# Causal mask of the second attention: added on VectorE from PSUM instead of by two matmuls on TensorE

## The chip, the cores and the metric

The kernel runs on one core of one Trainium2 chip. The metric is the time of one execution on the device in microseconds (us); lower is better. Before the change it is 649.9 us, the median of three runs (648.09 to 652.0).

## The reference

The input x has 128 sequences of 32 tokens with 256 features. Two layers follow one another. The first is an attention with 16 heads and no mask, behind an RMS norm that is scaled and shifted by a condition, with normalised q and k. The second takes its output as the hidden state h and computes this (the second attention is the one with the causal mask):

```
x1     = rmsnorm(h, ln1_w)
scores = einsum("bqhd,bkhd->bhqk", q(x1), k(x1)) / sqrt(16)
scores = where(tril(ones(32, 32)), scores, finfo.min)
probs  = softmax(scores)
attn   = einsum("bhqk,bkhd->bqhd", probs, v(x1)) @ Wo.T
mod    = 0.1 * tanh(attn @ A)
u      = rmsnorm(h, ln2_w)
gate   = silu(u @ W_in.T + mod * (u @ A) @ B)
out    = x + h + (gate * (u @ W_up.T)) @ W_down.T
```

## The kernel before

Tokens are taken in 16 blocks of 256 (two tiles of 128 tokens, t = 0 and 1; a tile holds four sequences). Most products are made of three matmuls, with each operand split into a high and a low part. Names tell the part of the work: `x_` loads and normalises, `a_` is the first attention, `o_` and `r_` its output and residual, `b_` the second attention, `m_` its modulation, `f_` the gated network in four pairs of chunks (0 to 3), and `h`, `l` in tile names stand for high and low.

Nothing is planned at run time. Three lists written out by hand give the order: START (blocks 0 to 3 fill up), ORDER (the body of the loop over positions 4 to 13, each entry with a shift: -1 is the block before), and END. Each engine walks through the same list and takes the entries that are its own, so an engine's queue is strictly in that order, and an entry that waits holds all behind it on its engine. Semaphores `done[name]` count the entries that are finished. TensorE (PE) and SyncE (SP) have the lists unrolled.

The second attention of a block goes like this. PE makes q and k (`b_q`, `b_k`) into the two PSUM banks `b_banks`, ScalarE (ACT) copies them out (`b_q_out`, `b_k_out0` to `3`). `b_scores` on PE first multiplies an identity in bf16 (`identb`) with a mask in bf16 (`maskb`) into both banks, 512 columns each (line 657), and then adds 64 small matmuls onto it (line 506). VectorE (DVE) runs `b_shift1` and `b_shift0`, each for one tile: the maximum over the keys (line 911) and the difference from it (line 914), both read from PSUM, the second into `zb` in SBUF. ACT takes the exponential in place (`b_exp`, line 858), DVE the sum and its reciprocal (`b_rowsum`, lines 919 and 921), GpSimd (POOL) scales by it (`b_weigh`, line 1118), DVE transposes (`b_flip`, line 925), and `b_pv` on PE (line 671) multiplies with the values `vj`. These were moved across partitions before: `b_v_out1` on ACT (lines 853 and 854) ends the copy of the values, and `b_move` on SP then issues 16 DMAs (line 469). `m_turn` on PE (line 680) writes into the second of the banks and waits for both `b_shift`.

Around it in ORDER, in the queues of the single engines: on PE `f_gate2`, `b_scores`, (next position) `a_turn1`, `a_turn0`, `f_up2`, `f_down0`, `f_gate3`, `a_v`, `a_scores`, `f_up3`, `f_down1`, `f_down2`, `b_pv`, `x_turn`, `f_up0`, `a_pv0`. On ACT `f_tanh2`, `x_norm1`, `b_v_out1`, `f_hi1`, `a_k_out0`, `b_exp1`, `a_k_out3`, `b_exp0`, `a_k_out2`, `x_norm0`, `a_k_out1`, `a_q_out`, `f_tanh3`, `f_hi2`. On DVE `f_half2`, `b_shift1`, `b_shift0`, `b_rowsum1`, `b_rowsum0`, `f_mul2`, `b_flip1`, `b_flip0`, `f_half3`, `a_shift1`. On POOL `f_lo1`, `b_weigh1`, `b_weigh0`, `f_lo2`, where `f_lo` (line 1123) subtracts the high part from the product, from SBUF to SBUF. `a_scores` (line 506 too, into `a_banks`) waits for `a_q_out` and the four `a_k_out`.

A few more lines of DVE that the text speaks of: line 1075 `f_half`, 1082 `f_mul`, 1039 `o_lo` and 1063 in `m_mul` (both read two tensors in SBUF).

Of the kernel before, what the change touches and what calls it, by code (L numbers as in the profile page):

```python
# [44 lines left out]
    ("a_flip0", 0), ("m_mul", -1), ("a_pv0", 0), ("a_pv1", 0), ("x_scale", 1), ("m_turn", -1), ("x_shift", 1),  # L45
    ("o_odd", 0), ("m_out", -1), ("o_even", 0), ("f_down3", -2), ("o_hi", 0), ("f_gate0", -1), ("x_hi", 1),
# [35 lines left out]
    ("a_weigh0", 1), ("r_add", 0), ("b_weigh1", 0), ("masks", 0), ("b_weigh0", 0), ("lo", 9), ("lo", 10),  # L82
    ("a_shift1", 1), ("b_exp1", 0), ("a_v_out", 1), ("b_exp0", 0), ("load", 2), ("x_shift", 2), ("x_lo", 2),
    ("hi", 11), ("a_shift0", 1), ("a_rowsum1", 1), ("b_v0", 0), ("load", 3), ("a_scale1", 2), ("a_scale0", 2),
    ("a_rowsum0", 1), ("b_shift0", 0), ("b_shift1", 0), ("a_flip1", 1), ("a_flip0", 1), ("hi", 12), ("o_odd", 1),
    ("load", 4), ("b_v1", 0), ("x_square", 3), ("b_scores", 0), ("o_hi", 1), ("load", 5), ("m_tanh", 0),
# [100 lines left out]
def bass_adaln_attention_ffn(nc, x, condT, w_emb, b_emb, g_norm, w_qkv, gq, gk, w_out, ln1, ln2,  # L187
# [5 lines left out]
    with ExitStack() as ctx:  # L193
# [11 lines left out]
        wdn = [sb(f"wdn_{s}", [P, FC, D], F32R) for s in ("hi", "lo")]  # L205
        b3 = sb("b3", [96, FF], F32R)
        ident = sb("ident", [P, P])
        identb = sb("identb", [P, P], BF16)
        causal = sb("causal", [P, S])
        maskb = sb("maskb", [P, H, S], BF16)  # L210
        heads = sb("heads", [P, 8])
# [960 lines left out]
```

## Time and profile before

| what | value |
|---|---|
| median of 3 runs | 649.9 us |
| profiled execution | 646.44 us, of it 644.6 us span from first to last instruction |
| mean granted TensorE clock | 0.973 of full speed |
| PE busy | 600.9 us (93%) |
| DVE busy | 462.1 us (72%) |
| ACT busy | 370.0 us (57%) |
| POOL busy | 221.1 us (34%) |
| chain that ended last | PE 75%, issue of DMAs by SP 10%, DVE 6% |

The busy time of an engine is the sum of its instructions. The chain is followed back from the last instruction, at each step to what released it. The loop runs from about 142 to 536 us, with a distance of about 35.9 us from one position to the next.

### The profile page before, as it was taken

What the parts mean: (1) busy time and instruction counts of PE and PEld (TensorE: products, weight loads), DVE (VectorE), ACT (ScalarE), POOL (GpSimd) and SP (SyncE); (2) the same over time, 40 slices, a digit from 0 to 9 for tenths busy, and PEclk for the clock granted to TensorE, in tenths of its full rate; (3) what the DMA queues carried; (4) which work ended last, traced back from release to release, by engine and by line L of the source; (5) the groups of instructions that cost most, each with busy time, mean ns of one, the idle gap of its engine ahead of it and who ended that gap; (6) DMA issues with size and microseconds to landing.
All of it is one profiled execution on the core that took longest, in us unless ns stands there. A gap on an engine that the chain in (4) does not pass through costs nothing.

```text
span 644.6 us, 22549 instructions
## 1 busy us (share of the span) xinstructions
PE 600.9 (93%) x9112; PEld 558.6 (87%) x9128; DVE 462.1 (72%) x1070; ACT 370.0 (57%) x803; POOL 221.1 (34%) x196
## 2 busy tenths in 40 slices
PE   9565789899999999999999999999999999999997
PEld 8544679788999999999999999999999998888997
DVE  4567878577686777777786767777787766976452
ACT  3647656474565748475665747474656657473531
POOL 1221323415153443424242444334242533523132
PEclk9956799899999999999999999999999999999999
DMA  6322200000201002010101001010101010010000
GB/s 181 90 82 82 71 20 23 14 21 17 67 18 49 19 4 60 11 53 16 50 18 51 19 14 50 8 56 13 51 18 50 18 35 15 7 39 15 27 25 34
DMA packets 31961, 24.35 MB, mean 38 GB/s; under 512 B 7632, under 2 KB 30800, under 8 KB 31872
## 3 DMA queue, kind: packets, MB, share of 16 engines
q1 hardware_dynamic: 31328, 22.36, 11.8%
q8 instruction: 73, 1.20, 0.8%
q10 hardware_dynamic: 544, 0.66, 0.4%
q14 instruction: 16, 0.13, 0.1%
HBM read 14.61 MB, written 4.19 MB: 29 GB/s over the span
## 4 chain that ended last, share of the span: by engine, by line
PE 75%; SPq 10%; DVE 6%; issue 4%; ACT 2%; DMA 2%; POOL 1%; POOLq 0%; ACTq 0%; DVEq 0%
PE gate_bank L494 12%; PE up_bank L494 11%; PE down_bank L718 10%; SPq L469 10%; PE b_banks L494 7%; PE a_banks L486 7%; PE x_bank L486 6%; PE a_banks L609 4%; PE b_banks L486 3%; PE b_banks L506 2%; PE gate_bank L704 2%; PE a_banks L506 2%; PE up_bank L533 2%; DMA vj<-vs 2%; PE b_banks L671 2%
## 5 line engine op out<-in xcount | busy, mean ns | idle before, releaser
L1123 POOL TENSOR_TENSOR gl<-gu,gh 128x512 fp32r<-128x512 f32 x64 | 83.1, 1299 | 117.9 <-ACT gh L877 117.7
L1075 DVE SCALAR_TENSOR_TENSOR th<-th,gate_bank 128x512 f32<-128x512 f32 x64 | 43.2, 675 | 46.8 <-ACT th L872 46.8
L494 PE MATMUL up_bank<-uh,wup_hi 128*128 128x256 f32 x256 | 76.3, 298 | 0.0
L1111 POOL TENSOR_TENSOR qk<-qk,rx 128x512 f32<-128x512 f32 x32 | 33.3, 1060 | 123.6 <-DVE rx L903 123.6
L718 PE MATMUL down_bank<-wdn_hi,gh 128*128 128x256 f32 x256 | 74.1, 290 | 0.6 <-POOL gl L1123 0.6
L494 PE MATMUL gate_bank<-uh,win_hi 128*128 128x256 f32 x256 | 72.4, 283 | 0.2
L718 PE MATMUL down_bank<-wdn_hi,gl 128*128 128x256 f32 x256 | 72.1, 282 | 0.0
L718 PE MATMUL down_bank<-wdn_lo,gh 128*128 128x256 f32 x256 | 72.1, 282 | 0.0
L494 PE MATMUL up_bank<-ul,wup_hi 128*128 128x256 f32 x256 | 71.9, 281 | 0.0
L494 PE MATMUL up_bank<-uh,wup_lo 128*128 128x256 f32 x256 | 71.9, 281 | 0.0
L494 PE MATMUL gate_bank<-ul,win_hi 128*128 128x256 f32 x256 | 71.4, 279 | 0.0
L494 PE MATMUL gate_bank<-uh,win_lo 128*128 128x256 f32 x256 | 71.4, 279 | 0.0
L1118 POOL TENSOR_TENSOR za<-za,ria 128x512 f32<-128x512 f32 x32 | 33.0, 1051 | 80.5 <-DVE ria L921 80.5
L872 ACT ACTIVATE th<-gate_bank 128x512 f32<-128x512 f32 x64 | 38.3, 598 | 37.7 <-PE gate_bank L704 34.6
L877 ACT ACTIVATE gh<-gu 128x512 fp32r<-128x512 f32 x64 | 40.3, 631 | 27.7 <-DVE gu L1082 19.6
L494 PEld LDWEIGHTS up_bank<-uh,wup_hi 128*128 128x128 f32 x256 | 48.8, 191 | 2.7 <-issue 2.5
L1082 DVE TENSOR_TENSOR gu<-th,up_bank 128x512 f32<-128x512 f32 x64 | 42.9, 670 | 9.4 <-PE up_bank L494 6.6
L718 PEld LDWEIGHTS down_bank<-wdn_hi,gh 128*128 128x128 f32 x256 | 48.3, 189 | 1.4 <-POOL gl L1123 0.9
L494 PEld LDWEIGHTS gate_bank<-uh,win_hi 128*128 128x128 f32 x256 | 48.2, 188 | 1.4 <-issue 0.8
L494 PEld LDWEIGHTS up_bank<-ul,wup_hi 128*128 128x128 f32 x256 | 49.0, 191 | 0.0
L494 PEld LDWEIGHTS up_bank<-uh,wup_lo 128*128 128x128 f32 x256 | 48.7, 190 | 0.0
L494 PEld LDWEIGHTS gate_bank<-ul,win_hi 128*128 128x128 f32 x256 | 48.1, 188 | 0.4
(157 smaller groups left out, 1844.4 us busy)
## 6 DMA issues: line engine op xcount, KB each, us to landing
xa<-in_x SPq DMA_DIRECT2D x16, 256.0 KB, 3.6
xres<-in_x SPq DMA_DIRECT2D x16, 256.0 KB, 2.9
vj<-vs SPq DMA_DIRECT2D x256, 16.0 KB
out<-outb SPq DMA_DIRECT2D x16, 256.0 KB, 3.2
stage<-in_w_inT SPq DMA_DIRECT2D x2, 512.0 KB, 3.6
stage<-in_w_upT SPq DMA_DIRECT2D x2, 512.0 KB, 4.2
stage<-in_w_downT SPq DMA_DIRECT2D x2, 512.0 KB, 4.0
stage<-in_w_qkv SPq DMA_DIRECT2D x2, 384.0 KB, 4.9
```

The costliest lines, as they stand in the source:

```text
L469: sp.dma_start(vj[32 * j:32 * j + 32, b].rearrange("p t r -> p (t r)"), vs2[32 * b:32 * b + 32, u].rearrange("p t r -> p (t r)")).then_inc ...
L486: mm = pe.matmul(dst, stat[a][:, k, t * P:(t + 1) * P], w[b][:, k, c0:c1], start=(k == 0 and j == 0), stop=(k == KT - 1 and j == 2))
L494: mm = pe.matmul(dst, w[a][:, k, c0:c0 + P], mov[b][:, k, :], start=(first and k == 0 and j == 0), stop=(last and k == KT - 1 and j == 2), ...
L506: mm = pe.matmul(place(t, m, b, g), stat(t, m)[rows, 32 * b:32 * b + 32], mov(t, m)[rows, P * b:P * b + P], start=start, stop=True, skip_g ...
L718: mm = pe.matmul(Db[:, t * D:(t + 1) * D], stat[a], wdn[b][:, 2 * c + i, :], start=(c + t + i + j == 0), stop=(c == PAIRS - 1 and i == 1 a ...
L872: act.activation(th[:, :, :].rearrange("p c n -> p (c n)"), Gb[:, :], ACT.Tanh, scale=0.5).then_inc(f_tanh, 1)
L877: act.activation(gh[:, c % 2], gu[:, c % 2], ACT.Copy).then_inc(f_hi, 1)
L1075: dve.scalar_tensor_tensor(out=whole, in0=whole, scalar=1.0, in1=Gb[:, :], op0=ALU.add, op1=ALU.mult).then_inc(f_half, 1)
L1082: dve.tensor_tensor(gu[:, c % 2].rearrange("p c n -> p (c n)"), th[:, :, :].rearrange("p c n -> p (c n)"), Ub[:, :], ALU.mult).then_inc(f_ ...
L1111: pool.tensor_tensor(heads_of, heads_of, rx[:, 32 * t:32 * t + 32].unsqueeze(2).to_broadcast([P, 2 * H, HD]), ALU.mult).then_inc(done[name ...
L1118: pool.tensor_tensor(z[:, t], z[:, t], ri[:, t, :].unsqueeze(2).to_broadcast([P, H, S]), ALU.mult).then_inc(done[name], 1)
L1123: pool.tensor_tensor(gl[:, c % 2], gu[:, c % 2], gh[:, c % 2].bitcast(F32), ALU.subtract).then_inc(f_lo, 1)
```

## The change

The two mask matmuls of `b_scores` go, with `identb`, `maskb` and the entry `masks` that filled them. All matmuls of the scores now overwrite (`start=True`). A new entry `b_mask0` or `b_mask1` stands on DVE directly in front of each `b_shift` in all three lists. It adds `causal` (float32, broadcast over the heads) to the scores as it reads them from PSUM and writes `zb`. `b_shift` then takes the maximum of `zb` and subtracts it in place, from SBUF to SBUF. `m_turn` waits for the two `b_mask` and no longer for the two `b_shift`. No other entry changes its place.

```diff
 ORDER = [
-    ("x_load", 2), ("x_norm1", 1), ("f_half2", -2), ("b_v_out1", -1), ("a_turn1", 0), ("b_shift1", -1),
-    ("f_hi1", -2), ("b_move", -1), ("a_turn0", 0), ("f_up2", -2), ("a_k_out0", 0), ("f_lo1", -2), ("b_shift0", -1),
+    ("x_load", 2), ("x_norm1", 1), ("f_half2", -2), ("b_v_out1", -1), ("a_turn1", 0), ("b_mask1", -1),
+    ("b_shift1", -1), ("f_hi1", -2), ("b_move", -1), ("a_turn0", 0), ("f_up2", -2), ("a_k_out0", 0), ("f_lo1", -2),
+    ("b_mask0", -1), ("b_shift0", -1), ("b_exp1", -1), ("f_down0", -2), ("a_k_out3", 0), ("b_rowsum1", -1),
...
-                    for bank in range(2):
-                        pe.matmul(Bb[:, bank, :], identb[:, :], maskb[:, :, :].rearrange("p h s -> p (h s)"),
-                                  start=True, stop=False, skip_group_check=True)
                     scores(b_place, lambda t, m: q2T[:, m, t, :],
-                           lambda t, m: k2p[:, m, t].rearrange("p b h s -> p (b h s)"), False).then_inc(done[name], 1)
+                           lambda t, m: k2p[:, m, t].rearrange("p b h s -> p (b h s)")).then_inc(done[name], 1)
...
-                    wait(pe, done["b_shift0"], n)
-                    wait(pe, done["b_shift1"], n)
+                    wait(pe, done["b_mask0"], n)
+                    wait(pe, done["b_mask1"], n)
...
+                if name[2:-1] == "mask":
+
+                    wait(dve, done["b_scores"], n)
+                    wait(dve, done[f"b_flip{t}"], n - 1)
+                    if isinstance(n, int) and n == 0:
+                        dve.wait_ge(loaded["causal"], 16)
+                    dve.tensor_tensor(z[:, t].rearrange("p (g c) s -> p g c s", g=4), sc(t),
+                                      causal[:, :].unsqueeze(1).unsqueeze(1).to_broadcast([P, 4, H // 4, S]),
+                                      ALU.add).then_inc(done[name], 1)
+                elif name == f"b_shift{t}":
+                    wait(dve, done[f"b_mask{t}"], n)
+                    dve.tensor_reduce(mx[:, t, :], z[:, t], AX_X, ALU.max).then_inc(maxed[x][t], 1)
+                    wait(dve, maxed[x][t], n)
+                    dve.tensor_tensor(z[:, t], z[:, t], mx[:, t, :].unsqueeze(2).to_broadcast([P, H, S]),
+                                      ALU.subtract).then_inc(done[name], 1)
```

## Rows read from the trace of the kernel before

**Rows 1.** Busy time by windows: length, busy PE, PEld, DVE, ACT, POOL, PE clock, DMA.

```profile
357.10:393.10 36.00, 35.73 (x565) 33.41 (x566) 27.05 (x64) 22.15 (x49) 13.96 (x13) 1.00 0.10 32
```

**Rows 2.** Chain of waits, a position of the loop: start, duration, engine and work.

```profile
365.79 1.09 PE a_banks L506 x64
...
371.33 0.67 PE b_banks L671 x52
```

**Rows 3.** Chain of waits, the position three before.

```profile
250.83 0.08 ACT ha L854
...
261.88 1.76 DMA vj<-vs
...
263.77 0.73 PE b_banks L671 x50
```

**Rows 4.** Timeline of SP, the DMAs of b_move: start, duration of the group.

```profile
215.25 10.76 SPq L469 DMA_DIRECT2D vj<-vs  x16
...
250.97 11.51 SPq L469 DMA_DIRECT2D vj<-vs  x16
...
358.75 10.81 SPq L469 DMA_DIRECT2D vj<-vs  x16
...
502.37 10.89 SPq L469 DMA_DIRECT2D vj<-vs  x16
```

**Rows 5.** Timeline of PE's weight loads around the mask.

```profile
357.13 0.12 PEld L657 LDWEIGHTS b_banks<-maskb,identb 128*128 128x128 bf16 x2
357.67 0.92 PEld L506 LDWEIGHTS b_banks<-k2p,q2T 64*32 64x32 f32 x64 [0.42 <-issue]
```

**Rows 6.** Groups by form on DVE: count, then busy, mean ns, idle before.

```profile
L914 DVE TENSOR_TENSOR zb<-b_banks,mxb 128x512 f32<-128x512 f32 x32 | 22.1, 692 | 1.6
...
L911 DVE TENSOR_REDUCE mxb<-b_banks 128x16 f32<-128x512 f32 x32 | 21.9, 684 | 8.3 <-PE b_banks L506 8.3
```

**Rows 7.** Timeline of DVE behind the scores.

```profile
357.96 0.69 DVE L1075 SCALAR_TENSOR_TENSOR th<-th,gate_bank 128x512 f32<-128x512 f32 x1 [1.59 <-ACT th L872]
358.93 0.69 DVE L911 TENSOR_REDUCE mxb<-b_banks 128x16 f32<-128x512 f32 x1 [0.29 <-PE b_banks L506]
359.66 0.69 DVE L914 TENSOR_TENSOR zb<-b_banks,mxb 128x512 f32<-128x512 f32 x1
360.27 0.68 DVE L911 TENSOR_REDUCE mxb<-b_banks 128x16 f32<-128x512 f32 x1
...
366.93 0.69 DVE L911 TENSOR_REDUCE mxa<-a_banks 128x16 f32<-128x512 f32 x1 [0.92 <-PE a_banks L506]
```

**Rows 8.** Timeline of ACT in the same stretch.

```profile
361.71 0.63 ACT L858 ACTIVATE zb<-zb 128x512 f32<-128x512 f32 x1
...
363.79 0.69 ACT L792 ACTIVATE q1T<-a_banks,gcol 128x512 f32<-128x512 f32 x1
```

**Rows 9.** Timeline of POOL in the same stretch.

```profile
359.27 1.29 POOL L1123 TENSOR_TENSOR gl<-gu,gh 128x512 fp32r<-128x512 f32 x1 [1.27 <-ACT gh L877]
```

**Rows 10.** Timeline of POOL and of DVE, an earlier stretch.

```profile
158.41 2.99 POOL L1123 TENSOR_TENSOR gl<-gu,gh 128x512 fp32r<-128x512 f32 x2 [3.36 <-ACT gh L877]
...
158.74 1.50 DVE L1039 TENSOR_TENSOR ol<-o,oh 128x512 fp32r<-128x512 f32 x1
```

**Rows 11.** Single lines of DVE: duration ns min/median/max, first and last start.

```profile
L1063 DVE SCALAR_TENSOR_TENSOR m<-th,ha x16: 181/652/1273, 83.1 to 618.9; 128x32 f32<-128x32 f32 x16
...
L1039 DVE TENSOR_TENSOR ol<-o,oh x16: 648/693/1575, 44.4 to 589.3; 128x512 fp32r<-128x512 f32 x16
```

**Rows 12.** Chain of waits behind the loop.

```profile
541.34 0.70 DVE mxb L911
...
550.54 0.87 PE a_banks L609 x53
```

**Rows 13.** Timeline of DVE and of PE behind b_pv.

```profile
372.72 0.71 DVE L925 STREAM_TRANSPOSE pTa<-za 128x512 f32<-128x512 f32 x1 [0.17 <-POOL za L1118]
...
373.89 0.31 PE L609 MATMUL a_banks<-pTa,vs 32*32 32x64 f32 x12
```

More of the change, by code:

```diff
@@ L35 @@
 ORDER = [
[9 rows of a table removed]
-    ("a_flip0", 0), ("m_mul", -1), ("a_pv0", 0), ("a_pv1", 0), ("x_scale", 1), ("m_turn", -1), ("x_shift", 1),
-    ("o_odd", 0), ("m_out", -1), ("o_even", 0), ("f_down3", -2), ("o_hi", 0), ("f_gate0", -1), ("x_hi", 1),
[7 rows of a table removed]
[10 rows of a table added]
+    ("m_turn", -1), ("x_shift", 1), ("o_odd", 0), ("m_out", -1), ("o_even", 0), ("f_down3", -2), ("o_hi", 0),
+    ("f_gate0", -1), ("x_hi", 1), ("o_lo", 0), ("x_lo", 1), ("r_mm", 0), ("f_tanh0", -1), ("f_half0", -1),
+    ("a_qk1", 1), ("f_mul0", -1), ("r_square", 0), ("a_qk0", 1), ("r_rms", 0), ("a_square1", 1), ("a_copy1", 1),
+    ("f_gate1", -1), ("f_hi0", -1), ("f_lo0", -1), ("r_norm0", 0), ("r_norm1", 0), ("f_out", -2), ("a_sum1", 1),
+    ("r_load", 0), ("r_turn", 0), ("f_up1", -1), ("f_store", -2), ("r_hi", 0), ("f_tanh1", -1), ("r_lo", 0),
[4 rows of a table added]
 ]
@@ L81 @@
     ("ld_b_emb", 0), ("x_load", 2), ("ld_wo_a", 0), ("a_exp0", 1), ("b_v_out1", 0), ("a_weigh1", 1), ("ld_g", 0),
[L82 to L85, printed above, removed]
@@ L86 @@
-    ("load", 4), ("b_v1", 0), ("x_square", 3), ("b_scores", 0), ("o_hi", 1), ("load", 5), ("m_tanh", 0),
-    ("f_lo0", 0), ("x_load", 3), ("a_v", 1), ("x_turn", 2), ("load", 6), ("x_hi", 2), ("ld_causal", 0),
-    ("b_rowsum1", 0), ("b_rowsum0", 0), ("lo", 11), ("a_pv0", 1), ("a_pv1", 1), ("f_up0", 0), ("b_flip1", 0),
-    ("b_flip0", 0), ("o_even", 1), ("x_scale", 2), ("o_lo", 1), ("r_square", 1), ("a_weigh0", 2), ("a_square0", 2),
-    ("a_weigh1", 2), ("load", 7), ("m_out", 0), ("r_norm1", 1), ("r_norm0", 1), ("lo", 12), ("a_copy1", 2),
@@ L91 @@
-    ("load", 8), ("r_hi", 1), ("a_square1", 2), ("m_mul", 0), ("r_rms", 1), ("f_tanh0", 0), ("a_copy0", 2),
-    ("b_k_out1", 1), ("a_sum0", 2), ("r_add", 1), ("r_lo", 1), ("a_sum1", 2), ("b_pv", 0), ("r_mm", 1),
[8 rows of a table removed]
-    ("r_load", 0), ("r_turn", 1), ("b_rowsum0", 1), ("o_even", 2), ("o_odd", 2), ("a_scale1", 3), ("f_gate0", 0),
[4 rows of a table removed]
-    ("m_tanh", 1), ("load", 12), ("a_copy0", 3), ("a_copy1", 3), ("m_out", 1), ("f_lo1", 1), ("x_load", 4),
-    ("b_move", 0), ("a_weigh0", 3), ("vd_zero", 0), ("r_square", 2), ("x_norm0", 4), ("x_norm1", 4), ("a_rms", 3),
@@ L108 @@
-    ("f_up2", 0), ("a_v", 2), ("f_gate3", 0), ("r_load", 1), ("x_turn", 3), ("f_down0", 0), ("f_up3", 0),
-    ("b_weigh1", 2), ("f_down1", 0), ("a_pv0", 2), ("a_pv1", 2), ("a_qk1", 3), ("r_rms", 2), ("a_qk0", 3),
-    ("f_half0", 1), ("f_out", 0), ("b_pv", 1), ("x_lo", 4), ("f_down2", 0), ("r_lo", 2), ("f_tanh0", 1),
[7 rows of a table removed]
+    ("a_weigh0", 1), ("r_add", 0), ("b_weigh1", 0), ("b_weigh0", 0), ("lo", 9), ("lo", 10), ("a_shift1", 1),
+    ("b_exp1", 0), ("a_v_out", 1), ("b_exp0", 0), ("load", 2), ("x_shift", 2), ("x_lo", 2), ("hi", 11),
@@ new lines @@
+    ("a_shift0", 1), ("a_rowsum1", 1), ("b_v0", 0), ("load", 3), ("a_scale1", 2), ("a_scale0", 2),
+    ("a_rowsum0", 1), ("b_mask0", 0), ("b_shift0", 0), ("b_mask1", 0), ("b_shift1", 0), ("a_flip1", 1),
+    ("a_flip0", 1), ("hi", 12), ("o_odd", 1), ("load", 4), ("b_v1", 0), ("x_square", 3), ("b_scores", 0),
+    ("o_hi", 1), ("load", 5), ("m_tanh", 0), ("f_lo0", 0), ("x_load", 3), ("a_v", 1), ("x_turn", 2), ("load", 6),
+    ("x_hi", 2), ("ld_causal", 0), ("b_rowsum1", 0), ("b_rowsum0", 0), ("lo", 11), ("a_pv0", 1), ("a_pv1", 1),
@@ new lines @@
+    ("f_up0", 0), ("b_flip1", 0), ("b_flip0", 0), ("o_even", 1), ("x_scale", 2), ("o_lo", 1), ("r_square", 1),
+    ("a_weigh0", 2), ("a_square0", 2), ("a_weigh1", 2), ("load", 7), ("m_out", 0), ("r_norm1", 1), ("r_norm0", 1),
+    ("lo", 12), ("a_copy1", 2), ("load", 8), ("r_hi", 1), ("a_square1", 2), ("m_mul", 0), ("r_rms", 1),
[10 rows of a table added]
+    ("b_rowsum0", 1), ("o_even", 2), ("o_odd", 2), ("a_scale1", 3), ("f_gate0", 0), ("b_k", 1), ("b_q", 1),
[5 rows of a table added]
+    ("vd_zero", 0), ("r_square", 2), ("x_norm0", 4), ("x_norm1", 4), ("a_rms", 3), ("f_up2", 0), ("a_v", 2),
[10 rows of a table added]
@@ L497, in feature_major, with scores @@
                 return mm
-            def scores(place, stat, mov, start):
+            def scores(place, stat, mov):
                 for t in range(TB):
@@ L506, in scores @@
                                 mm = pe.matmul(place(t, m, b, g), stat(t, m)[rows, 32 * b:32 * b + 32],
[L507 removed]
+                                               mov(t, m)[rows, P * b:P * b + P], start=True, stop=True,
                                                skip_group_check=True)
@@ L1030, in do @@
                     softmax(name, n, "a", a_scores_of, za, pTa, mxa, rsa, ria)
-                elif name[:2] == "b_" and name[2:-1] in ("shift", "rowsum", "flip"):
+                elif name[:2] == "b_" and name[2:-1] in ("mask", "shift", "rowsum", "flip"):
                     softmax(name, n, "b", b_scores_of, zb, pTb, mxb, rsb, rib)
```

28 lines of the change are left out of this document (9 added, 19 removed), and 112 rows, old and new, of tables (END, ORDER, START).

## The prediction

> **What bounds the kernel now.** I read the busy time by windows first. In one position of the loop PE is busy for 35.73 of 36.00 us at full clock, DVE for 27.05, ACT for 22.15 and POOL for 13.96 [rows 1]. That looks like a kernel that is bound by PE alone, so that whatever is taken off PE would be gained. The chain of waits says something narrower. In one position it runs through PE from end to end, and `b_pv` (line 671) follows the matmuls before it at 371.33 [rows 2]. Three positions earlier it leaves PE: it goes from the last copy of the values on ACT (250.83) through SP's 16 issues, and the DMA that starts at 261.88 and takes 1.76 us ends just before `b_pv` at 263.77 [rows 3]. So there are two chains of nearly one length between the scores and `b_pv`. The SP timeline says how near. The 16 issues take 10.76, 10.81 or 10.89 us in some positions and 11.51 in others [rows 4]; of the nine groups from 215.25 to 502.37, five are short ones and four long ones, in turn. The issues of rows 3 end at 250.97 + 11.51 = 262.48, and `b_pv` starts 1.29 us later. I measure both chains from the start of the mask's weight load, m = 357.13 [rows 5]. PE reaches `b_pv` at m + 14.20 [rows 2]. The DMA chain starts at m + 1.62 [rows 4] and allows `b_pv` at 1.62 + 10.81 + 1.29 = m + 13.72 in a short position, at 1.62 + 11.51 + 1.29 = m + 14.42 in a long one. The DMA chain begins with the copies on ACT that queue behind `f_tanh2`, which waits for `f_gate2`, the work of PE just in front of the mask. The mask matmuls are therefore not in that chain, and removing them doesn't shorten it.
>
> **PE, what goes.** The mask's weight loads start at 357.13 and those of the scores at 357.67 [rows 5]: 0.54 us for each block, 16 x 0.54 = 8.6 us in all. If no wait took its place, the short positions would gain 14.20 - 13.72 = 0.48 us each and the long ones nothing, 5 x 0.48 = 2.4 us, since the DMA chain then sets `b_pv`. That is the most that the loop can gain. The 64 score matmuls stay as they are; that they overwrite instead of adding I cost at nothing, as the same line into `a_banks` does it at the same rate.
>
> The Trainium skill (TensorE: Matmul & The Clock Gate, section "Wait — 56ns, not 53.3ns?") gives 215.7 ns from start to start for 512 columns at full clock, by which the two would be an estimated 0.43 us and not 0.54, or 6.9 us for 16 blocks; the sum would hardly move, as little of it is gained either way.
>
> **DVE, what comes.** Before, a tile takes a maximum and a difference, 684 and 692 ns [rows 6], with 0.73 us from the start of the one to that of the other, which waits for it, and 0.61 to the next tile [rows 7]. After, a tile is sum, maximum, difference. The sum reads PSUM and one SBUF tensor like the old difference: 0.69. Maximum and difference now read SBUF: the nearest row for an operation with both operands there is `o_lo`, median 693 ns, minimum 648 [rows 11]; I take 0.69 again, 0.65 and 0.72 bound it. One more step of 0.72 for each tile, 1.4 us for a block, on an engine that idles for about 9 us of 36 [rows 1]. On load alone this is free. What counts is who waits behind it.
>
> The Trainium skill (VectorE: DVE Perf Modes, section "The TRN2 errata") has a table with 58 fixed cycles for a source in SBUF and 120 for one in PSUM. By it maximum and difference would get some 0.06 us shorter each, an estimated 0.25 us for a block, or 4 us of DVE time in all. The median of 693 ns from SBUF beside 692 from PSUM [rows 6, 11] speaks against it.
>
> **A lock that the difference now meets.** The old difference read PSUM and took 692 ns whatever POOL did. Line 1039, which reads two SBUF tensors, has a maximum of 1575 ns beside its median of 693 [rows 11]. One such case: it starts at 158.74, with POOL's line 1123 at work since 158.41; at 1.29 us each [rows 9] the first of the two POOL operations ends at 159.70, and the DVE one ends at 160.24, 0.54 us later, as if it had run only then [rows 10]. Line 1063, on 32 elements, takes 181 ns at best and 652 in the median for the same reason. The new difference reads `zb` and `mxb`, two SBUF tensors. The Trainium skill (SBUF — State Buffer, section "SBUF: two separate sides") tells of a port pair of VectorE and GpSimd that one holds for its whole instruction when VectorE reads two SBUF tensors. The trace agrees, with those numbers.
>
> **The loop, step by step.** `f_half2` runs at 357.96 as before, since `f_tanh2` holds it, and the next DVE operation can start 0.61 later. So `b_mask1` starts at 358.57 and not at 358.93 - 0.54 [rows 7]: 0.36 us of PE's 0.54 arrive here. Maximum at 359.30. The difference wants 360.02, but POOL's `f_lo1` runs from 359.27 to 360.56 [rows 9], and it ends at 361.11. Then `b_mask0` at 361.03, maximum 361.76, difference 362.48 to 363.17. `b_exp0` on ACT started at 361.71 [rows 8]; now at 363.20, 1.49 us later. Behind it in ACT's queue stand `a_k_out2`, `x_norm0`, `a_k_out1` and `a_q_out`, which ended at 363.79 + 0.69 = 364.48 [rows 8] and now ends at 365.97. PE's `a_scores` waits for these. Its weight loads started 0.08 before 365.79 [rows 2], at 365.71; now at 366.03 at the earliest, 0.32 later, although PE could be there 0.54 earlier. This is the wait that takes the place of the mask. `b_pv` then comes at m + 14.20 + 0.32 = 14.52 by PE. Short positions: 14.52 for 14.20, +0.32. Long ones: 14.52 for 14.42, +0.10. 5 x 0.32 + 4 x 0.10 = +2.0 us for the loop. The bounds: without the lock the difference of the second tile ends 0.47 earlier, `a_scores` starts 0.15 before its old time, and the loop gains 5 x 0.15 = 0.8 us.
>
> What the later DVE work does: `b_rowsum1` and all up to `f_half3` come about 1.5 us later, of which the 0.92 us that DVE waited for `a_scores` at 366.93 [rows 7] swallows most; `a_shift1` starts some 0.5 late. `a_flip0` ended at 372.72 + 0.71 = 373.43, and PE's `a_pv0`, which waits for it, started at 373.89 [rows 13]: 0.46 of cover, and PE itself is 0.32 late, so I cost this at nothing. `b_weigh` on POOL, `f_lo2` and `f_tanh3` come 1.5 late with their users further off. `m_turn` waits for less than before; at nothing. SP issues the same DMAs, and nothing moves past them.
>
> **The first blocks.** Block 1's mask stands with nothing but PE around it and is worth up to 0.54 us, of which the later transposes give about half back. In block 0 the scores are done before DVE comes to them, so all of its 1.4 us is added to a full queue; about 0.6 gets through. Bounds -1.1 (two blocks' 0.54) to +1.4; I take +0.3, nearer the middle because both go through the same DVE. The entry `masks` that goes had no one waiting on it: nothing.
>
> **The last blocks.** Behind the loop the chain runs through DVE, from the first `b_shift` of block 13 at 541.34 on to `a_pv0` at 550.54 [rows 12], through the six steps in place of four: +1.4, less the 0.54 by which PE lets DVE start earlier: +0.9. In block 15 DVE meets no POOL operation, and `f_mul2` behind the softmax comes 1.4 - 0.36 = 1.0 later; `f_up3` on PE, which waits for it and has some 0.7 of cover, is about 0.35 late. Together +1.2; bounds 0 and +2.8.
>
> **Sum.** +2.0 + 0.3 + 1.2 = +3.5 us. The sum is made against the profiled execution: 646.44, which is its span of 644.6 and 1.8 around it, becomes 649.9. The median of the runs lies 3.5 us above that execution; I carry this distance over, and 649.9 becomes 653.4 us. A measurement of this kernel tells about 0.5% (3.2 us) from no change, so the forecast stands on that edge.
>
> **The rivals.**
> - *PE's time is gained* (faster). It needs `b_pv` to have no DMA chain behind it and `a_scores` no ACT queue: 649.9 - 8.6 = 641.3. The point from which it decides: 16 issues in under 13.66 - 1.62 - 1.29 = 10.75 us in every position, and DVE's six steps done before 362.3. Rows 3 and 4 speak against it: 0.04.
> - *The lock doesn't hit the difference* (POOL and DVE don't meet, or the new form isn't held). Loop -0.8, ends +1.5: +0.7, 650.6: 0.17.
> - *DVE becomes the pace.* `a_flip0` or `f_mul3` runs out of cover: if DVE is 0.5 us later than I reckon, with 0.46 of cover at `a_pv0` [rows 13] partly spent, some 0.3 us comes on top in each of 10 positions, and as much in the ends: +6.5 to +8, 657: 0.17.
> - *The change doesn't shorten PE's queue* (the slot of the mask fills with the start of the scores). The loop is held by `a_q_out` anyway; the ends lose 0.5 to 1 more: 654.2: 0.04.
> - The forecast, 651.0 to 655.5, has the remaining 0.58.
>
> **How the numbers follow.** Of the forecast's 0.58 some 0.28 lies within 0.5% and 0.30 above. Faster: 0.04 + 0.01 = 0.05. Same: 0.28 + 0.16 = 0.44. Slower: 0.30 + 0.17 + 0.04 = 0.51. The range takes in the forecast, the case without the lock and most of the DVE case: 649.0 to 657.5.
>
> **What the profile would show.** `b_pv` 14.5 us behind the start of the scores' block in all positions, and no longer in turn 14.2 and 14.4. A wait of PE for ACT's `q1T` of about 0.8 us in each position. The difference of the first tile at 1.1 us and that of the second at 0.69. If the first is 0.69 too, the lock step is wrong. If PE waits for `vj` and not for `q1T`, the ACT step is wrong. If the period falls by 0.5 us, the DMA chain was no bound.

## The result, and the profile of the changed kernel

The changed kernel is slower by 1.3%: 657.8 us in the median (653.8 to 662.8) beside 649.0 for the kernel before, ratio 1.0127 with an interval of 1.0086 to 1.0168. Run again beside the last experiments it gave 659.8 us and 1.0167 (1.013 to 1.0205). The sign was forecast, the size was not: 3.5 us were reckoned, and 8.8 came, 11.2 in the repetition. At the ratio of the first measurement the forecast's 649.9 us becomes 658.2, just above the range's upper end of 657.5.

The profiled execution took 658.1 us, of it 656.3 us span, at a mean granted clock of 0.964. The page of the changed kernel, busy times and the chain that ended last:

```profile
PE 600.6 (92%) x9096; PEld 561.2 (86%) x9096; DVE 485.2 (74%) x1100; ACT 370.6 (56%) x803; POOL 221.8 (34%) x196
...
PE 66%; DVE 17%; issue 7%; ACT 6%; POOL 2%; SPq 2%; DMA 0%; ACTq 0%; POOLq 0%; DVEq 0%
```

DVE has 23 us more work, as reckoned, and PE is busy as long as before although the mask matmuls are gone; more of its work ran at half clock (the mean granted clock was 0.973 before). The chain has changed hands: PE and SP's issues have given up 9 and 8 points of it, and DVE's share went from 6% to 17%. One position of the loop by windows (the columns of [rows 1]):

```profile
328.00:364.00 36.00, 35.11 (x564) 33.14 (x562) 28.86 (x66) 22.23 (x49) 13.75 (x13) 1.00 0.11 31
```

PE now lacks 0.9 us of 36 where it lacked 0.3. The three DVE steps of a tile, groups by form (count, busy, mean ns of one, idle before), answer to [rows 6]:

```profile
L916 DVE TENSOR_TENSOR zb<-zb,mxb 128x512 f32<-128x512 f32 x32 | 26.6, 830 | 1.1
L914 DVE TENSOR_REDUCE mxb<-zb 128x16 f32<-128x512 f32 x32 | 22.0, 687 | 1.1
L909 DVE TENSOR_TENSOR zb<-b_banks,causal 128x512 f32<-128x512 f32 x32 | 21.8, 682 | 3.8 <-PE b_banks L507 3.8
```

Sum and maximum take what was put in for them. The difference takes 830 ns in the mean, and the timeline says why. DVE and POOL in the loop, which answer to [rows 7] and [rows 9]:

```profile
365.42 0.68 DVE L909 TENSOR_TENSOR zb<-b_banks,causal 128x512 f32<-128x512 f32 x1
366.12 1.29 POOL L1129 TENSOR_TENSOR gl<-gu,gh 128x512 fp32r<-128x512 f32 x1 [1.27 <-ACT gh L873]
366.13 0.69 DVE L914 TENSOR_REDUCE mxb<-zb 128x16 f32<-128x512 f32 x1
366.86 1.10 DVE L916 TENSOR_TENSOR zb<-zb,mxb 128x512 f32<-128x512 f32 x1
...
369.31 0.69 DVE L916 TENSOR_TENSOR zb<-zb,mxb 128x512 f32<-128x512 f32 x1
```

The first difference lasts until 367.96, 0.55 us past the end of POOL's operation; the second has no such neighbour. In nine of the ten positions, blocks 4 to 12, the first one is 0.40 to 0.42 longer than 0.69. The chain of waits through the same position, from there to `b_pv`, and the waits of PE and of its weight loads over the whole span (us, times, longest):

```profile
370.04 0.04 ACT zb L854
...
372.22 0.59 ACT q1T L788
...
372.85 1.16 PE a_banks L507 x64
...
378.46 0.67 PE b_banks L667 x51
```
```profile
PEld a_banks L507 <- ACT q1T L788: 9.2, 11, 0.9
PE a_banks L507 <- ACT q1T L788: 7.0, 11, 0.7
```

The scores' weight loads begin at 364.07 here, so `a_scores` comes 8.78 us and `b_pv` 14.32 us after them. (This `b_pv` is the start of its first matmul in the timeline, 378.39. The chain counts it from the end of the matmul ahead, 378.46.) In the kernel before, the same distances from the mask's load were 8.58 and 14.1 to 14.5 in turn. Now they are 8.78 and 14.29 to 14.34 for all blocks from 4 to 12 (8.41 and 13.94 for block 3, whose difference met no POOL operation).

Something else in that chain was in no step of the forecast. Behind `b_pv`, in the middle of the 128 small matmuls of `a_pv`:

```profile
381.93 0.72 PE a_banks L610 x45
382.65 0.95 issue
383.61 0.34 PE a_banks L610 x13
383.95 0.35 PE b_banks L676 x2
384.31 2.42 PE down_bank L714 x12
```

PE stands for 0.95 us with nothing to wait for that the profile shows, and then runs twelve matmuls in 2.42 us that take 1.41 at full clock, as the granted clock fell to 0.5 for 3.41 us. Such stalls stand in five of the ten positions (3.1 us in all), this half clock behind one of them.

To tell where the time went I cut each trace at two places: the scores' first weight load of block 3, and that of block 13 (in kernels with mask matmuls the mask's load, 0.54 us earlier). The ten positions between are split once more, at the first matmul of each `b_pv`. The column `a_pv` says what the ten runs of `a_pv` last together beyond 1.77 us each, which an undisturbed one takes from its first matmul to its last. In us, one profiled execution of each kernel:

```
kernel                            until    ten         up to   from    a_pv   rest    span
                                  block 3  positions   b_pv    b_pv
before                            177.7    358.7       142.6   216.1   0.4    108.2   644.6
changed                           181.7    366.3       142.8   223.5   4.2    108.3   656.3
changed, again                    181.2    367.4       144.0   223.4   2.3    108.3   656.9
mask matmuls kept, DVE adds too   180.5    368.2       144.5   223.7   1.9    109.8   658.5
no mask at all                    175.3    361.3       137.8   223.5   4.4    106.5   643.1
no mask, values copied early      175.0    358.3       136.4   221.9   2.5    106.5   639.8
changed, difference from PSUM     178.1    365.8       139.5   226.4   5.9    108.4   652.3
changed, other order on DVE       179.4    362.5       141.9   220.6   2.7    107.9   649.8
changed, late exponential         179.0    378.6       139.2   239.4   5.7    108.2   665.9
changed, two small matmuls        181.0    363.1       145.6   217.5   0.4    110.1   654.2
other order and small matmuls     180.5    364.0       147.4   216.6   0.6    109.8   654.4
before, values copied early       182.9    356.5       140.8   215.7   0.2    107.4   646.8
changed, values copied early      183.2    361.8       139.5   222.3   2.8    108.2   653.1
the same, PE's program moved      187.5    359.7       139.5   220.2   0.6    108.6   655.8
```

The rest is as before. The loop has 7.6 to 8.6 us more, where 2.0 were reckoned. The forecast reckoned the path up to `b_pv`, and there the changed kernel has 0.2 us more than before (1.4 in the repetition). All else, 7.4 us, is lost behind `b_pv`, and the kernel with no mask at all loses as much there (223.5 for 216.1), without any new work on DVE. (The kernel with both mask forms loses 7.6 us there, but 5.0 of them by a wait of its own.) The first blocks have 4 us more, but their length is no fixed thing: the kernel before, changed only in when it copies the values, has 182.9 there with longer stretches at half clock.

### The profile page after: what moved, and what is told of

Read it like the earlier page. It is cut to its first block, busy times and chain, and to the rows that moved or that the text cites. A ratio compares the mean times of both kernels' runs of the same rounds, so it can differ in the third digit from the quotient of the medians.

```text
span 656.3 us, 22531 instructions
## 1 busy us (share of the span) xinstructions
PE 600.6 (92%) x9096; PEld 561.2 (86%) x9096; DVE 485.2 (74%) x1100; ACT 370.6 (56%) x803; POOL 221.8 (34%) x196
## 4 chain that ended last, share of the span: by engine, by line
PE 66%; DVE 17%; issue 7%; ACT 6%; POOL 2%; SPq 2%; DMA 0%; ACTq 0%; POOLq 0%; DVEq 0%
PE gate_bank L495 10%; PE up_bank L495 10%; PE down_bank L714 10%; PE b_banks L495 7%; PE a_banks L487 6%; PE x_bank L487 4%; PE a_banks L610 4%; DVE mxb L914 3%; DVE zb L909 3%; PE b_banks L487 3%; PE a_banks L507 2%; ACT k1p L797 2%; PE gate_bank L700 2%; PE up_bank L534 2%; SPq L470 2%
## 5 line engine op out<-in xcount | busy, mean ns | idle before, releaser
L1124 POOL TENSOR_TENSOR zb<-zb,rib 128x512 f32<-128x512 f32 x32 | 34.0, 1080 | 53.6 <-DVE rib L932 53.6
L495 PEld LDWEIGHTS gate_bank<-uh,win_lo 128*128 128x128 f32 x256 | 49.2, 192 | 0.0
```

Of the source, the lines that this page charges most:

```text
L495: mm = pe.matmul(dst, w[a][:, k, c0:c0 + P], mov[b][:, k, :], start=(first and k == 0 and j == 0), stop=(last and k == KT - 1 and j == 2), ...
L1124: pool.tensor_tensor(z[:, t], z[:, t], ri[:, t, :].unsqueeze(2).to_broadcast([P, H, S]), ALU.mult).then_inc(done[name], 1)
```

## The experiments

**Only the DVE half.** The two mask matmuls go back in front of the scores, and DVE still adds.

```diff
+                    for bank in range(2):
+                        pe.matmul(Bb[:, bank, :], identb[:, :], maskb[:, :, :].rearrange("p h s -> p (h s)"),
+                                  start=True, stop=False, skip_group_check=True)
                     scores(b_place,
```

> The DVE part alone: the two mask matmuls stay in PE's queue (the scores then overwrite them), DVE adds the mask as in the changed kernel. Theory A (two causes: the wait of a_scores for a_q_out, and stalls of PE inside a_pv that come from where PE's program is cut, as it is 4 instructions a block shorter): PE's program is as in the kernel before, so the long gaps inside a_pv (0.5 to 1.2 us in every second block of the changed kernel) are gone; b_exp0 starts where it did in the changed kernel, since POOL's f_lo1 holds the first difference to the same moment; distance of the positions even, 36.0 us, loop +1 us on before, whole 650 to 653 us, ratio 1.002 to 1.007. Theory B (DVE's later work makes those gaps too): the gaps stay, the loop is as long as in the changed kernel or longer, ratio 1.012 to 1.02.

661.3 us, ratio 1.0203 (1.0157 to 1.025). It is the slowest but two of all. Theory B had a loop and a ratio like these, but neither theory had the place. The chain of waits shows a place that nobody had looked at, the last step of the norm of the residual (`r_rms`), and the timeline shows its neighbour:

```profile
354.99 0.17 DVE nr_t L902
355.17 0.02 issue
355.19 1.29 DVE rr L906
...
356.50 0.48 ACT tok L830
```
```profile
355.17 1.28 POOL L1141 TENSOR_TENSOR gl<-gu,gh 128x512 fp32r<-128x512 f32 x1 [3.88 <-ACT gh L880]
355.19 1.28 DVE L906 SCALAR_TENSOR_TENSOR rr<-nr_t,nr_y 128x2 f32<-128x2 f32 x1
```
```profile
PE x_bank L630 <- ACT tok L830: 5.0, 5, 1.2
```

An operation on two columns, 0.17 us otherwise, takes 1.28 because a POOL operation began 0.02 us before it, and PE waits for the result in every second position, 5.0 us in all (the last line, waits of PE from 180 to 540 us). So what the later DVE work costs depends on which short steps it pushes into POOL's operations. Two more things went against theory A. The stalls inside `a_pv` are still there in two positions (blocks 4 and 12) although PE's program is as long as before. And as the scores come 0.54 us later, the first difference meets only the end of POOL's operation: it takes 0.69 to 0.73 us in the loop and not 1.1.

**Only the PE half.** The mask matmuls go and nothing comes in their place.

```diff
-                    for bank in range(2):
-                        pe.matmul(Bb[:, bank, :], identb[:, :], maskb[:, :, :].rearrange("p h s -> p (h s)"),
-                                  start=True, stop=False, skip_group_check=True)
```

> The PE part alone: no mask matmuls and no mask on DVE; b_shift reads PSUM as before. The kernel leaves the causal mask out. Theory A: the short positions gain up to 0.5 us and the long ones nothing (DMA chain to b_pv), at most -2.4 us in the loop, but the gaps inside a_pv are there as in the changed kernel, +3 us or more with what they cost in clock: 647 to 652 us. Theory B: no gaps inside a_pv, loop -2.4 us, ends -1 to -2: 645 us, ratio 0.992 to 0.996. The count by PE alone would be -8.6 us: 640.5 us.

648.0 us, 0.9987 (0.995 to 1.0024): of PE's 8.6 us nothing that can be measured arrives. The chain of waits has the DMA of the values in front of `b_pv` again, and the waits of PE in the loop are these:

```profile
259.50 1.75 DMA vj<-vs
261.25 0.14 issue
261.39 0.73 PE b_banks L666 x50
```
```profile
PE a_banks L609 <- issue: 2.8, 4, 1.0
PE b_banks L666 <- DMA vj<-vs: 0.9, 3, 0.3
```

The first line of the waits is the stall inside `a_pv`. It comes with no DVE change at all.

The DMA chain is not what takes PE's gain, though. The scores of this position start here:

```profile
247.45 0.65 PEld L506 LDWEIGHTS b_banks<-k2p,q2T 64*32 64x32 f32 x47
```

`b_pv` comes 13.94 us behind them, in a position for which the forecast had the DMA chain hold it at 14.42. From block 4 on no group of the 16 issues takes more than 11.13 us, where four took 11.3 to 11.6 before; why is not shown. Over the ten positions 4.8 of PE's 5.4 us arrive at `b_pv` (137.8 for 142.6), and PE waits for the DMA for 0.9 us. Then 7.4 us are lost behind `b_pv`, 4.0 of them inside `a_pv` and some 1.4 by a half clock behind a stall. Of the expectation, theory A's time and stalls are right, and its 2.4 us at most for the loop is too little: undisturbed distances are 35.3 to 35.7 us where they were 35.7 to 36.1.

**The same with the values copied early**, `b_v_out1` directly behind `b_q_out`, so that SP can issue some 1 us sooner; and **the kernel before with that alone**.

```diff
-    ("b_v_out1", -1), ("a_turn1", 0),
+    ("a_turn1", 0),
...
-    ("b_q_out", 0), ("b_scores", 0),
+    ("b_q_out", 0), ("b_v_out1", 0), ("b_scores", 0),
```

> The PE part alone (no mask matmuls, no mask on DVE; the causal mask is left out) with b_v_out1 early as in the run before. If the DMA chain ate PE's gain: each position is 0.54 us shorter than in the run with the early b_v_out1 that keeps the mask matmuls, 35.2 us, less what the gaps in a_pv take (about 3 us in the loop); 5 us less than that run without them, 2 us less with them. If the DMA chain was not what ate it: 35.7 us as there.

> The kernel before with one edit: b_v_out1 stands right behind b_q_out in ACT's queue and no longer behind f_tanh2, so that the DMA chain to b_pv starts about 1.5 us earlier. If that chain is what holds b_pv in the long positions: no wait for vj, even positions of 35.7 us, loop 1 to 1.5 us shorter, ratio 0.997 to 0.999. If not: no change.

Without mask: 641.9 us, 0.99 (0.9848 to 0.9951), undisturbed distances of 35.2 us. With the mask as before: 648.8 us, 0.9975 (0.9938 to 1.0012), and ten distances of 35.6 to 35.8 where they had gone from 35.7 to 36.1. The even distances show the DMA chain: with it they go in turn, without it they don't, and the loop of the kernel before is 2.2 us shorter without it. By the medians the mask on PE is worth 0.75% with that chain out of the way (0.99 against 0.9975) and 0.1% with it, but the intervals overlap, so the two are not told apart. The traces say that the mask's time arrives at `b_pv` either way (4.4 us without the chain, 4.8 with it) and is lost behind it either way (6.2 and 7.4 us). So in the profiled executions the loop with neither mask nor chain is 1.8 us longer than that with the mask, where 2 to 5 us less were expected.

**The lock taken away by the operand.** The difference reads the scores from PSUM again, the sum still runs.

```diff
-                    dve.tensor_tensor(z[:, t], z[:, t], mx[:, t, :].unsqueeze(2).to_broadcast([P, H, S]),
+                    dve.tensor_tensor(z[:, t].rearrange("p (g c) s -> p g c s", g=4), sc(t),
+                                      mg.unsqueeze(3).to_broadcast([P, 4, H // 4, S]),
```

> The changed kernel with the difference read from PSUM and not from zb, so that it has only one tensor in SBUF; m_turn waits for the two b_shift again. The array that is added is all zeros, so the causal mask is left out; the same instructions run. If POOL's f_lo1 holds the difference because that reads two SBUF tensors: it takes 0.69 us right behind the maximum and not 1.1 to 1.7, a_scores starts 0.4 us earlier (8.35 us behind the start of the scores and not 8.78), the loop is 1 to 2 us shorter than in the changed kernel. If something else held it: same place as in the changed kernel. The gaps inside a_pv stay in both.

654.5 us, 1.0079 (1.0052 to 1.0107). Groups by form:

```profile
L917 DVE TENSOR_TENSOR zb<-b_banks,mxb 128x512 f32<-128x512 f32 x32 | 22.1, 692 | 1.1
```

692 ns where it was 830, `a_scores` 8.37 us after the scores instead of 8.78, and PE's wait for `q1T` in the loop 2.8 us instead of 6.6. The stalls inside `a_pv` stay (3.7 us). The loop was to be 1 to 2 us shorter than in the changed kernel and is 0.5 shorter: 3.3 us are gained up to `b_pv`, and 2.9 are lost behind it, where eight of the ten `a_pv` last 2.05 to 3.18 us and not 1.77.

**The lock taken away by the order.** DVE runs sum and maximum of both tiles first (both stand in `b_mask` here), then both differences.

```diff
-    ("b_mask1", -1), ("b_shift1", -1), ..., ("b_mask0", -1), ("b_shift0", -1),
+    ("b_mask1", -1), ("b_mask0", -1), ("b_shift1", -1), ..., ("b_shift0", -1),
```

> The changed kernel with DVE's six steps in another order: sum and maximum of the one tile, sum and maximum of the other, then the two differences. The first difference then comes when POOL's f_lo1 is over and should take 0.69 us, no step waits for the one just before it except the maxima; b_exp0 starts about 0.6 us earlier, a_scores 8.2 us behind the start of the scores and not 8.78; 2 to 4 us shorter than the changed kernel, ratio 1.005 to 1.009. If the cost is in the number of steps alone and not in the meeting with POOL: within 1 us of the changed kernel.

653.1 us, 1.0056 (1.0024 to 1.0088). In the groups by form the difference takes 683 ns in the mean. `a_scores` comes 8.61 to 8.64 us after the scores, where 8.2 were expected. The loop is 3.8 us shorter than the changed one, but only 0.9 of it is gained up to `b_pv`; the other 2.9 are shorter stalls and no half clock.

So two different means take the lock away, and both kernels are faster than the changed one as it was measured again (1.013 to 1.0205); beside its first measurement (1.0086 to 1.0168) the intervals touch or overlap. What the lock alone costs in the whole is not shown. Positions without a stall keep their 35.9 to 36.1 us in both kernels: what `a_scores` gains, `a_pv` spends again, in gaps too short to be counted as stalls.

**The exponential of the second tile behind `a_q_out`.**

```diff
-    ("b_exp0", -1), ("f_gate3", -2), ...
+    ("f_gate3", -2), ... ("a_q_out", 0), ("b_exp0", -1),
```

> The changed kernel with b_exp0 behind a_q_out in the loop's order, so that the three copies that a_scores waits for no longer stand behind it. If the ACT queue is the wait: a_scores starts 8.1 us behind the start of the scores and PE no longer waits for q1T; b_pv then is held by the DMA chain alone, in turn 13.7 and 14.4 us; loop 1 to 2 us shorter than the changed kernel. If DVE is the pace: b_flip0 and a_flip0 come late, PE waits at a_pv for pTa, no gain or a loss.

666.5 us, 1.0257 (1.0216 to 1.0298). `a_scores` waits for ACT no more (8.01 us after the scores), so that step is right. The expected even `b_pv` at 13.7 and 14.4 us came at 13.6 to 14.1. But DVE's sum over the exponential is held, and all behind it; waits of PE over the span:

```profile
PE up_bank L496 <- DVE gu L1089: 14.1, 21, 1.1
```

This is the rival in which DVE becomes the pace, and it shows how near it lay: 1.1 us of wait at `f_up0` in a position.

**The number of PE's instructions.** Two matmuls of 16 columns ahead of each `b_scores`, which take the place of the mask matmuls in the program though not their time.

```diff
+                    for bank in range(2):
+                        pe.matmul(Bb[:, bank, 0:16], q2T[:, 0, 0, :], k2p[:, 0, 0, 0, 0, 0:16],
+                                  start=True, stop=True, skip_group_check=True)
                     scores(b_place,
```

> The changed kernel with two small matmuls of 16 columns in the place where the mask matmuls stood (the scores overwrite them), so that PE's program has as many instructions for a block as before the change. Theory A (the gaps of 0.5 to 1.2 us in the middle of a_pv come from where PE's program is cut into fetched pieces): the gaps at the same places are gone or moved to others; loop 3 us shorter than in the changed kernel unless they moved to a place that costs as much, ratio to before about 1.008. Theory B (they come from VectorE's side): nothing changes, ratio 1.012 to 1.015.

656.8 us, 1.0115 (1.0068 to 1.0162). In the timeline `a_pv` runs in one piece:

```profile
379.77 1.76 PE L610 MATMUL a_banks<-pTa,vs 32*32 32x64 f32 x127
```

The stalls inside `a_pv` are gone from the loop, and the profiled one is 3.2 us shorter. The median can't be told from that of the changed kernel, and 1.008 was expected. The edit does two things beside its purpose. As fp32, each small matmul has two records (PE has 9160 in the whole and not 9096), so the program is longer than before the change and not as long. And the scores come later, so that the first difference takes 0.73 to 0.82 us and not 1.1: most of the lock is gone too.

**Both together**, the other order on DVE and the small matmuls.

> The changed kernel with two edits at once: DVE's order mask and maximum, mask and maximum, difference, difference, and the two matmuls of 16 columns ahead of the scores. Theory A (the change's cost is a sum of three: the lock on the first difference, PE's stalls inside a_pv, and the added DVE work itself): the first two are gone, the rest is the base distance of about 36.0 us in the loop (10 x 0.13 = 1.3 us more than before) and what the first and last blocks add, some 1 to 3 us together; ratio to before 1.003 to 1.007, no wait of PE named issue inside a_pv, b_pv at 14.3 us from the scores' first weight load. Rival B (the stalls are paid elsewhere anyway, as in the run with the two small matmuls alone, whose ratio stayed at 1.0115): nothing beyond the new order is gained, the ratio is that of the new order or above it by the two matmuls' 0.2 us a block, 1.006 to 1.010.

656.3 us, 1.0099 (1.0065 to 1.0133): in rival B's range and outside theory A's, and no better than the order alone (1.0024 to 1.0088). The stalls in `a_pv` are gone, but the two small fp32 matmuls hold the scores back by 0.47 us (`a_scores` 9.09 us behind the first weight load instead of 8.62), nearly what the mask took, and the position of block 5 loses 0.6 us ahead of `b_pv`. The small matmuls are no free way to move a program.

**The changed kernel again, and with the values copied early.**

> The changed kernel itself once more, beside the two others on the same chip, for a direct comparison. Theory A (what the profile of the changed kernel showed belongs to the program): the first difference again takes 0.40 to 0.42 us longer in at least eight positions, the stalls of PE inside a_pv fall on the same blocks (5, 6, 8, 10, 12), a_scores at 8.78 and b_pv at 14.32 us from the scores' first weight load; ratio 1.009 to 1.017. Rival B (the stalls, the half clock behind one of them and the late first part were chance in that execution): the stalls fall on other blocks or none, and the sum of the ten distances of the loop is below 363 us.

> The changed kernel with b_v_out1 behind b_q_out, so that the DMAs of the values start about 1 us earlier. Theory A (in the changed kernel b_pv is set by the chain through ACT's a_q_out and PE's a_scores, at 14.3 us from the scores, and the DMA chain ended at 13.2 or 13.9 and is hidden): b_pv stays at 14.3 in undisturbed positions, the ratio to before stays at that of the changed kernel, 1.009 to 1.016. Rival B (the DMA chain still ends last now and then): the ratio falls by the 0.25 per cent or more that the same edit brought to the kernel before, to 1.010 or below, and the positions get even.

Again: 659.8 us. The lock is there in the same nine positions, `a_scores` and `b_pv` stand where they stood in all but three of them, and the loop sums to 367.4. The stalls inside `a_pv`, though, are two and not five, in blocks 4 and 12, and the half clock is behind the second. Their place is not fixed by the program alone, and both theories are right in part only. Nor is the loop shorter with fewer stalls: PE waits 0.9 us for `vj` in block 5 and 0.9 us for DVE's `xres` once.

Copied early: 655.1 us, 1.0095 (1.0056 to 1.0135), and an undisturbed distance of 35.63 us, as in the kernel before with the same edit (35.62). The ratio lies in both theories' ranges, but `b_pv` was to stay at 14.3 us by theory A and came at 13.95. DVE and POOL in a position show what it overlooked:

```profile
364.36 1.29 POOL L1145 TENSOR_TENSOR gl<-gu,gh 128x512 fp32r<-128x512 f32 x1 [0.93 <-ACT gh L889]
364.73 0.69 DVE L930 TENSOR_REDUCE mxb<-zb 128x16 f32<-128x512 f32 x1
365.45 0.76 DVE L932 TENSOR_TENSOR zb<-zb,mxb 128x512 f32<-128x512 f32 x1
```

With `b_v_out1` out of ACT's queue, `f_hi1` ends earlier, POOL starts 1.09 us ahead of the difference and not 0.74, and the lock shrinks from 0.41 to 0.07 us here, and to 0.04 in the mean of all 32 differences, where it was 0.14. An ACT entry with no tie to the softmax decided what the DVE step cost.

**PE's program moved as a whole**, on top of that: 20 matmuls of 16 columns ahead of PE's very first.

```diff
+                    if not shifted:
+                        shifted.append(1)
+                        for _ in range(20):
+                            pe.matmul(Ub[0:96, 0:16], mt[:, 0, :], mt[:, 0, 0:16], start=True, stop=True)
```

> The changed kernel with b_v_out1 behind b_q_out (no lock, base distance 35.63 us) and 20 matmuls of 16 columns ahead of the very first ones of PE, where it has nothing to do but wait: they only move the rest of PE's program by 40 instructions. Theory A (the stalls inside a_pv are PE waiting for its own instructions: in the kernels with the shorter program each stall ended 2.3 to 2.8 us after a transfer of 16 KB on the instruction queue had begun, and the transfer began 0.05 us before a_pv at 381.02 in the changed kernel, but 0.93 us before it at 373.89 in the kernel before, where no stall followed): with the program moved by about as much as the mask matmuls of nine blocks had moved it, the transfers begin earlier against a_pv; the stalls of blocks 8 and 12 (1.15 and 1.07 us, and the half clock behind the first, 1.7) are gone or fall on other blocks, the ten distances of the loop sum to 357.5 to 359.5 instead of 361.8, ratio to before 1.002 to 1.006. Rival B (the place in the program has nothing to do with it: the stalls come from what other engines do at that time, or from how many matmuls stand before the scores): the stalls stay in blocks 8 and 12, sum 361 to 363, ratio 1.008 to 1.011.

661.2 us, 1.0213 (1.0182 to 1.0244), outside both theories. PE wasn't idle there, and the timeline shows what the added ones cost (they count double, as fp32, so the program moved by some 80 instructions and not 40):

```profile
1.12 6.58 PE L554 MATMUL up_bank<-mt 128*96 128x16 f32 x40 [1.12 <-DVE mt L963]
```

All first blocks come that much later, which spoils the ratio. The loop is still readable: no stall in `a_pv`, no half clock, a sum of 359.7 instead of 361.8, just above theory A's 359.5. What points to a cause of the stalls is the view of the DMA queues in a short window. First the changed kernel from 380.90 to 381.05, where `a_pv` starts at 381.02 and stalls, then the kernel before from 372.90 to 373.05, where it starts at 373.89 and doesn't (queue, kind: packets, MB, share):

```profile
q8 instruction: 1, 0.02, 50.0%
```
```profile
q8 instruction: 1, 0.02, 40.2%
```

A block of 16 KB of instructions is on its way. In all 14 traces together there are 38 stalls behind the 100th us (over 0.4 us from one weight load of `a_pv` to the next, with nothing waited for), and each of them ended 2.20 to 2.90 us after such a transfer had begun. In every stall of 0.85 us or more in the loop the transfer began within 0.4 us of the start of `a_pv`; in the kernel before, where none is in the loop, it begins 0.9 us or more ahead of that start or 1.0 us behind it. Five runs of `a_pv` in the kernels with moved programs have a transfer within 0.4 us of their start too and no stall, and so has the `a_pv` of block 2 in eight of the others, so that the moment alone doesn't decide.

## Why the prediction was right in its sign and short in its size

**PE's time is not gained: right in the outcome, wrong in the reason.** The kernel without any mask is at 0.9987 (0.995 to 1.0024), so nothing that can be measured arrives. The forecast had the DMA chain take it: at most 2.4 us for the loop, and none in the long positions. In the trace 4.8 us arrive at `b_pv`, in the long positions too, and 7.4 are lost behind it. The DMA chain is real, but it is a cost beside this one: without it the loop is 2.2 us shorter with the mask on PE (358.7 to 356.5) and 3.0 without (361.3 to 358.3). The rival's 641.3 us is near what the kernel with neither mask nor chain takes (641.9), by other terms than the rival's.

**DVE's added step: right.** 682, 687 and 690 ns for sum, maximum and undisturbed difference, beside 0.69. The Trainium skill (VectorE: DVE Perf Modes, section "The TRN2 errata") would have the reads from SBUF shorter by an estimated 0.06 us; the maximum took 687 ns from SBUF and 684 from PSUM, so no run here shows it.

**The lock: right, and now shown.** +0.41 for a forecast of +0.43 (1.09 in all from 360.02 to 361.11, measured 1.10). It goes when the operand is in PSUM and when the order changes, and nearly so when POOL comes earlier or the scores later. Its price in the loop was put at 2.8 us (+2.0 with it, -0.8 without). Without it 3.3 and 0.9 us are gained up to `b_pv`, but the undisturbed distance stays, so that price is not shown. The Trainium skill (SBUF — State Buffer, section "SBUF: two separate sides") says that one engine holds the shared ports for its whole instruction; the trace agrees down to an operation on two columns that takes 1.28 us beside POOL's 1.28.

**The wait that takes the mask's place: right in kind, 0.12 us too long.** `a_scores` was put at m + 8.90 and `b_pv` at m + 14.52 in all positions; they came at 8.78 and, counted by the chain as the forecast does, 14.39, even in nine positions of ten as forecast. Up to `b_pv` the ten positions have 0.2 us more than before, where 2.0 were reckoned for nine. PE's wait for `q1T` was put at 0.8 and is 0.66. The undisturbed distance is 35.98 us. The forecast makes 36.07 of it (35.87 and 0.2), so this term was a little too high: in ten positions the undisturbed distance adds 1.1 us, most of it behind `b_pv`.

**The loop as a whole: +2.0 forecast, +7.6 and +8.6 measured. This is the step that failed.** The sum put all that follows `b_pv` in a position at nothing, and 7.4 of the 7.6 us lie there. By positions, 1.1 of the 7.6 are the undisturbed distance. The rest, 6.5 us, is what positions lose beyond 35.98: 5.7 us in the five positions with a stall in `a_pv` (4.2 of it in the gaps between the weight loads, some 1.5 by the half clock behind one), and 0.8 in block 3, where a last step of `r_rms` took 1.0 us too long beside POOL. Neither kind stands in the rivals. The stalls could have been asked for: the kernel before has one of 1.38 us at 115.79, in front of the loop. I had read PE's idle time in one clean position [rows 1] and taken the loop for ten of the same. I also took the gain side alone for PE's shorter program, when the shorter program moves where its instructions have to be loaded. That the transfer of instructions causes the stalls rests on the match in time and on the three kernels whose program was moved, which lost those in `a_pv` (and have one to three of 0.3 to 0.7 us in other runs of matmuls). Against a simple rule stand the kernel with both mask forms, whose program is as long as before and which has two, and the runs with a transfer and no stall. So the cause is made likely and not shown. What exactly decides between a stall and none was not settled, and the repetition, which had two where the first had five, shows that one program can have either.

**The first blocks: +0.3 forecast, some 4 measured, open.** The stretches at half clock in the first 100 us differ between executions of one kernel (the kernel before has mean clocks of 0.954 to 0.974 and takes 646.4 us in the median from 0.973 on, and 651.9 below 0.960). At clocks from 0.960 to 0.966 alone the medians are 649.1 us before and 658.5 changed, so the difference of the medians is not this. But how much of the 4 us in this one trace is DVE's work and how much the clock is not told apart.

**The last blocks: +1.2 forecast, +0.1 measured.** The path that was reckoned is right: from the scores of block 13 to `a_pv0` there are 14.94 us where there were 14.06 [rows 12], +0.9 as said. It is given back one block on. There the kernel before waits for SP's issues, and with them for the DMA of `b_pv` of block 14, two of the issues taking 1.66 and 1.57 us; from the scores of block 14 to those of block 15 it needs 29.99 us, and the changed kernel 28.73, where that chain isn't last. I followed the longer chain to its end in block 13 and not beyond.

**DVE becomes the pace: not as described.** `a_flip0` kept its cover, as PE doesn't wait for DVE's `pTa` in the loop. It is real one step further, as the run with the late exponential shows; in the one with both mask forms it is a short DVE step that POOL holds up.

## What to carry to other kernels

Matmuls taken off a full TensorE are not paid out by the path in front of them alone. Here 4.8 of 5.4 us arrived at `b_pv`, and 7.4 were lost behind it, with or without the new DVE work. Splitting the loop at such a point shows it; the DMA chain that ends there looked like the cause and was a cost of its own, 2 to 3 us. A new VectorE operation on two SBUF tensors is priced by the GpSimd operation that it meets, and so are all the short steps that it pushes along; 0.35 us of phase, given here by an unrelated copy on ACT, takes nearly all of the lock away. And before ten positions are reckoned as ten times a clean one, the worst position of the trace should be read, and its stalls named.

No variant with the mask on VectorE came up to the kernel before; the best of them, with the other order, is at 1.0056 (1.0024 to 1.0088), which is not told from the 1.0079 with the difference from PSUM. Copying the values early is the one edit that evened the loop in both kernels, at 0.9975 (0.9938 to 1.0012) for the kernel before, which is not told from no change.

## What the runs showed of the hardware beyond that

- TensorE can stand inside a run of small matmuls with nothing to wait for that the profile shows, for 0.4 to 1.5 us, ending 2.2 to 2.9 us after a 16 KB transfer on the instruction queue began; 128 such matmuls pass in 1.6 us otherwise.
- One stall of 0.95 us was followed by 3.41 us at a granted clock of 0.5. The same happened at or just behind a stall in five other kernels and in the repetition, not behind every stall.
- Forty records of 16-column fp32 matmuls, 20 in the program, at the head of the program took 6.58 us, 0.16 us each, so that fillers there are not free.
- An elementwise step on VectorE of two columns with two SBUF operands took 0.17 us alone and 1.28 us beside a GpSimd operation of 1.28 us.
